# Attention and experts in one block on one core: the experts' buffers over the attention's, batch 6 routed between two projections, the next batch's projections three places later

## The chip, the cores and the metric

One core of one Trainium2 chip runs the whole program. The metric is the device time of one execution in microseconds (us), as the median of repeated runs; lower is better. The core has five engines with their own instruction streams: TensorE (PE, with its weight loads shown apart as PEld), VectorE (DVE), ScalarE (ACT), GpSimd (POOL) and SyncE (SP), which here only issues DMAs. The streams meet at semaphores.

## The reference

Batches are counted from 0 to 7. Per batch, 256 image rows and 128 text rows of 256 numbers are the 384 tokens:

```python
h = tok(x)                       # 3x3 colour matrix, curve of 16 points, weighted sum, clip to 0..1
h = concatenate([h, txt], axis=1)            # (8, 384, 256)
h = h + attn(layernorm(h))
h = h + ffn(layernorm(h))
# attn: c = x W_DKV (64 wide); k = c W_UK; v = c W_UV; q = x W_UQ; 16 heads of 16
#       causal softmax(q k / 4) v, then W_O
# ffn:  router scores = softmax(x router_w), 8 experts, top 2 of each token;
#       each expert takes its first 384 tokens of the 1st choice and its first 384 of the 2nd,
#       y = gelu(xe w1[e]) w2[e] (256 -> 1024 -> 256), weighted by the score and added; plus bias
```

## The kernel before, in words

**Two blocks.** `build` makes the shared tensors and calls `front` (attention and routing of all eight batches) and then `experts`. Each of the two opens its own stack of SBUF buffers and its own `nc.Block()`, in which the five engines' programs stand. At the end of a block every engine drains and meets the others (line 131 of the profile, line 1405 at the end of the second block). The buffers of `front` are given back at its end, and `experts` takes the same memory.

**Turns.** `front` runs over turns `n` from -1 to 19, with `b = n // 2`: turns 2b and 2b+1 compute attention of batch b, half of the heads each (8 heads, four places `p` = 0 to 3 with two heads each). PE carries out, in place p of turn n: the scores of turn n+1 (`scores`, lines 579 and 580, read by DVE's row maxima, line 1081), the shifted transposed scores of turn n in three units (`shifted_scores`, lines 601 and 602, read by ACT's exponentials, lines 887 and 889), and at fixed places the sums with the values (`values`, 637), the contexts' transposes (`contexts_back` 649, `contexts_out` 656), W_O (`project`, 665, two pieces per batch, read by DVE's `residual`, 1115). The order of each engine is written out by hand; nothing is planned at build time.

**The next batch's chain.** Tokens of batch b+2 go through colours and curve (DVE 1124 to 1156, in places 0 and 1 of even turn 2b), layer norm (DVE `norms`, `variances`, the root on POOL at line 477, DVE `scaled` 1178 in place 3), transposes (`tokens_back`, PE 673, ACT 936: half 0 at the end of even turn 2b place 3, half 1 in place 0 of turn 2b+1), the latent (`latents`, 680, ACT 940, place 0), and for four half heads' worth of queries and keys `query_key` in three stages (PE 695 or 697, then 700 twice). Each stage waits for ACT's bf16 copy of the one before it (948); these copies go by DMA from SP into the stacked tensors `qs` and `ks` (358). All of it shares PSUM bank 1. Those stacks are first read by `scores` in turn 2b+3.

**Routing.** Batch b-2 is routed in turn 2b and 2b+1: `router` (PE 727) in place 1 of the even turn, `choose` on DVE (1207 to 1213), `mark` on DVE in place 2 (one-hot rows and running counts, 1224 to 1230), `ranks` on PE in place 3 (738, 739: how many earlier tokens chose the same expert), `keep_ranks` on DVE (1217), then in place 0 of the odd turn `weigh` (1239 to 1251) and `place` (1255 to 1261), which gives each token its two slots, and six indirect DMAs from POOL (`send`, 494) that write the token's row into `slot_rows` in DRAM. For batches 6 and 7 there is no attention beside it: turns 16 to 19 hold the rest, with `turning` (745), multiplications whose result nobody reads, between the steps. Batch 7's project and second layer norm run in turns 16 and 17 and batch 6's `weigh` and `place` follow them on DVE in turn 17.

**The experts.** Units u = 0 to 15 are (expert u // 2, choice u % 2). SP loads the 384 rows of a unit from `slot_rows` (1462), PE transposes them (1616), ACT and DVE split them into a high and a low float32r part (1537, 1582), PE multiplies by w1 (1630: high x high, low x high, high x low), ACT applies gelu twice (1542, 1545), DVE forms the low part (1588), PE multiplies by w2 (1645), ACT scales (1553), and POOL adds the rows to the output by indirect DMA (1511). The weights of expert 0 are loaded into `wr` during the attention; their high part is made by ACT (1560), their low part by DVE (1594) and POOL (1518); those of the later experts wholly on POOL (1496, 1499). SP loads unit 0's rows when all sends but batch 7's last three have landed (semaphores `sent`), unit 1's to 3's after those (`sent_last`). PE's program is `transpose_rows(0)`, `transpose_rows(1)` (which waits for DVE's `xl` of unit 0), then `hidden(0, f)`.

Of the kernel before, what the change touches and what calls it, by code (L numbers as in the profile page):

```python
# [11 lines left out]

# [53 lines left out]
RANK_STEP = 14  # L66
# [4 lines left out]
NMAT = MAT_WO + KC * DIM + KC * E  # L71

# [6 lines left out]
def build(nc, x, txt, params, mats, w1, w2, out):  # L79
# [3 lines left out]
    with ExitStack() as ctx:  # L83
        def sb(name, shape, dt=F32, where=None):
            return (where or ctx).enter_context(nc.sbuf_tensor(name, shape, dt))
# [6 lines left out]
        w_in = [ctx.enter_context(nc.semaphore(f"w_in{i}")) for i in range(2)]  # L92

        sent = [ctx.enter_context(nc.semaphore(f"sent{q}")) for q in range(2)]
        sent_last = ctx.enter_context(nc.semaphore("sent_last"))
        res_out = ctx.enter_context(nc.semaphore("res_out"))

        common = (ident, banks, s_bank, t_bank, sb)
        routed = (sent, sent_last, res_out)
        front(nc, common, wr, w_in, routed, x, txt, params, mats, w1, w2, slot_rows, out)  # L100
        experts(nc, common, wr, w_in, routed, w1, w2, slot_rows, out)


def front(nc, common, wr, w_in, routed, x, txt, params, mats, w1, w2, slot_rows, out):
# [8 lines left out]
    ident, banks, s_bank, t_bank, sb = common  # L113
# [17 lines left out]
    with ExitStack() as own:  # L131
        def buf(name, shape, dt=F32):
            return sb(name, shape, dt, own)

        def sem(name):
            return own.enter_context(nc.semaphore(name))

        hid = buf("hid", [P, B, NT, DIM])
        ident_b = buf("ident_b", [P, P], BF16)
        minus_b = buf("minus_b", [P, P], BF16)  # L140
        mask_q = buf("mask_q", [P, P], BF16)
        mask_k = buf("mask_k", [P, P], BF16)
        eps_t = buf("eps_t", [P, NT])
        neg_half = buf("neg_half", [P, NT])
        flag_f = buf("flag_f", [1, 2])
        flag_i = buf("flag_i", [1, 1], I32)
        prm = buf("prm", [P, NPRM])
        bias = prm[:, NPRM - DIM:NPRM]
        ccm_t = prm[:, 0:9]
        cbias = prm[:, 9:12]  # L150
        shift_t = prm[:, 12:60]
        slope_t = prm[:, 60:108]
        conv_t = prm[:, 108:111]
        convb_t = prm[:, 111:112]
        curve_w = buf("curve_w", [P, CH * PTS])
        minus_s = buf("minus_s", [P, CH])
        warm = buf("warm", [P, NT])
        less = buf("less", [P, MPARTS * HALF * T // P], BF16)
        mat = buf("mat", [P, NMAT])
        dkv = mat[:, 0:KC * P].rearrange("p (c n) -> p c n", c=KC)  # L160
        uq = mat[:, KC * P:KC * P + KC * DIM].rearrange("p (c n) -> p c n", c=KC)
        uk = mat[:, MAT_UK:MAT_UK + DIM]
        uv = mat[:, MAT_UK + DIM:MAT_WO]
        wo = mat[:, MAT_WO:MAT_WO + KC * DIM].rearrange("p (c n) -> p c n", c=KC)
        rw = mat[:, MAT_WO + KC * DIM:NMAT].rearrange("p (c e) -> p c e", c=KC)

        xin = [wr[q][:, 0:CH * IT * W].rearrange("p (c j w) -> p c j w", j=IT, c=CH) for q in range(2)]
        acc = wr[0][:, IT * W * CH:NW].rearrange("p (j w) -> p j w", j=IT)
        g = buf("g", [P, CH, IT, W])
        r = buf("r", [P, CH, IT, W])  # L170
        stats = buf("stats", [P, NT, 6])
        mv = buf("mv", [P, NT, 2])
        ve = buf("ve", [P, NT])
        rstd = buf("rstd", [P, NT])
        xn = buf("xn", [P, NT, DIM])
        xnT = buf("xnT", [P, KC, T])
# [149 lines left out]
        def bank_of(key):  # L326
            if key == "C":
                return C
# [1374 lines left out]
```

## Time and profile before

| what | us |
|---|---|
| median of 3 runs (716.57, 717.54, 721.19) | 717.54 |
| profiled execution, its own time | 715.48 |
| span of that execution in the trace | 713.6 |
| mean granted TensorE clock in it | 0.977 |

Times of rows are microseconds from the span's start. A row of a timeline has start, length, engine, line, operation, output and input, count, and in square brackets the idle time of the engine ahead of it with what ended it. PE rows overlap, since matmuls are pipelined.

### The profile page before, as it was taken

What the parts mean: (1) busy time and instruction counts of PE and PEld (TensorE: products, weight loads), DVE (VectorE), ACT (ScalarE), POOL (GpSimd) and SP (SyncE); (2) the same over time, 40 slices, a digit from 0 to 9 for tenths busy, and PEclk for the clock granted to TensorE, in tenths of its full rate; (3) what the DMA queues carried; (4) which work ended last, traced back from release to release, by engine and by line L of the source; (5) the groups of instructions that cost most, each with busy time, mean ns of one, the idle gap of its engine ahead of it and who ended that gap; (6) DMA issues with size and microseconds to landing.
All of it is one profiled execution on the core that took longest, in us unless ns stands there. A gap on an engine that the chain in (4) does not pass through costs nothing. (4 is left out here: it accounts for less than half of the span.)

```text
span 713.6 us, 14553 instructions
## 1 busy us (share of the span) xinstructions
PE 647.0 (91%) x5574; PEld 543.9 (76%) x5574; DVE 401.1 (56%) x1005; ACT 378.1 (53%) x800; POOL 303.8 (43%) x401
## 2 busy tenths in 40 slices
PE   2797999989899898999989869999999999999992
PEld 2555666666667666667767869999999999999992
DVE  4886685777867687648765144444444444444320
ACT  4365766747567485565661065545554444555540
POOL 3300001003121131030423659877788888888233
PEclk9999999999999998999999979999999999999997
DMA  7448392604333043153102252444444444442223
GB/s 256 112 117 227 89 271 69 198 32 137 106 83 113 9 113 90 44 151 128 63 24 76 76 202 66 104 104 104 105 104 105 104 104 104 105 104 46 24 29 37
DMA packets 66477, 73.76 MB, mean 103 GB/s; under 512 B 6312, under 2 KB 61458, under 8 KB 66408
## 3 DMA queue, kind: packets, MB, share of 16 engines
q1 hardware_dynamic: 55584, 59.27, 27.6%
q0 software_dynamic: 9504, 13.00, 10.7%
q8 instruction: 44, 0.72, 0.5%
q10 hardware_dynamic: 1320, 0.57, 0.3%
q14 instruction: 25, 0.20, 0.1%
HBM read 31.62 MB, written 22.35 MB: 76 GB/s over the span
## 5 line engine op out<-in xcount | busy, mean ns | idle before, releaser
L1588 DVE TENSOR_TENSOR hl<-h,hh 128x384 fp32r<-128x384 f32 x128 | 103.8, 812 | 155.2 <-ACT h L1545 155.2
L1081 DVE TENSOR_REDUCE mx<-s_bank 128x2 f32<-128x256 f32 (+2 forms) x192 | 124.4, 684 | 56.6 <-PE s_bank L580 55.5
L1542 ACT ACTIVATE hh<-t_bank 128x384 fp32r<-128x384 f32 x128 | 63.0, 492 | 132.5 <-PE t_bank L1630 130.2
L889 ACT ACTIVATE pt<-t_bank 128x512 f32<-128x512 f32 x128 | 76.5, 598 | 68.0 <-PE t_bank L602 65.4
L1511 POOL DMA_INDIRECT out<-yo,xr x48 | 75.1, 1564 | 71.3 <-ACT yo L1553 61.6
L1499 POOL TENSOR_TENSOR wl<-wr,wh 128x256 fp32r<-128x256 f32 x112 | 94.2, 875 | 1.2
L1630 PE MATMUL t_bank<-xh,wh 128*128 128x384 f32 x256 | 86.6, 338 | 0.0
L601 PE MATMUL t_bank<-qs,ks 98*128 98x384 bf16 (+2 forms) x384 | 85.7, 275 | 0.6 <-ACT pt L887 0.4
L1630 PE MATMUL t_bank<-xl,wh 128*128 128x384 f32 x256 | 86.2, 337 | 0.0
L1630 PE MATMUL t_bank<-xh,wl 128*128 128x384 f32 x256 | 86.0, 336 | 0.0
L579 PE MATMUL s_bank<-ks,qs 96*128 96x128 bf16 (+2 forms) x384 | 78.7, 274 | 5.0 <-DVE mx L1081 4.0
L494 POOL DMA_INDIRECT slot_rows<-row,slot_i x48 | 47.7, 994 | 71.6 <-ACT pt L889 58.3
L580 PE MATMUL s_bank<-mask_q,ident_b 128*128 128x128 bf16 x384 | 74.7, 220 | 0.0
L1645 PE MATMUL bank<-wh,hh 128*128 128x256 f32 x256 | 72.9, 285 | 0.0
L1645 PE MATMUL bank<-wh,hl 128*128 128x256 f32 x256 | 72.0, 281 | 0.0
L1645 PE MATMUL bank<-wl,hh 128*128 128x256 f32 x256 | 71.8, 281 | 0.0
L602 PE MATMUL t_bank<-mask_k,ident_b 128*128 128x128 bf16 x384 | 68.4, 220 | 0.0
L1545 ACT ACTIVATE h<-t_bank 128x384 f32<-128x384 f32 x128 | 62.4, 488 | 0.1
L475 POOL TENSOR_TENSOR ve<-mv,eps_t 128x3 f32<-128x3 f32 x8 | 1.5, 190 | 127.9 <-DVE mv L1171 127.9
L601 PEld LDWEIGHTS t_bank<-qs,ks 98*128 98x128 bf16 x384 | 37.8, 98 | 21.8 <-issue 5.3
L579 PEld LDWEIGHTS s_bank<-ks,qs 96*128 96x128 bf16 x384 | 37.5, 98 | 16.0 <-DVE mx L1081 4.6
L1630 PEld LDWEIGHTS t_bank<-xh,wh 128*128 128x128 f32 x256 | 48.9, 191 | 0.0
(191 smaller groups left out, 1451.8 us busy)
## 6 DMA issues: line engine op xcount, KB each, us to landing
wr<-in_w SPq DMA_DIRECT2D x16, 1024.0 KB, 5.8
qs<-part SPq DMA_DIRECT2D x96, 96.0 KB
ks<-part SPq DMA_DIRECT2D x90, 96.0 KB
slot_rows<-empty SPq DMA_DIRECT2D x4, 1560.0 KB, 9.1
xr<-slot_rows SPq DMA_DIRECT2D x16, 390.0 KB, 3.3
wr<-in_x SPq DMA_DIRECT2D x8, 768.0 KB, 5.6
out<-hid SPq DMA_DIRECT2D x8, 384.0 KB, 3.5
qs<-mT ACTq DMA_DIRECT2D x64, 3.0 KB
```

Of the source, the lines that this page charges most:

```text
L579: pe.matmul(dst, q[0:MROW, h, j * P:(j + 1) * P], k[0:MROW, h, 0:w], start=True, stop=False)
L580: mm = pe.matmul(dst[:, j * P:(j + 1) * P], ident_b[:, :], mask_q[:, :], start=False, stop=True)
L601: pe.matmul(bank[:, col:col + w], k[:, h, j * P:(j + 1) * P], q[:, h, j * P:T], start=True, stop=False)
L602: mm = pe.matmul(bank[:, col:col + P], ident_b[:, :], mask_k[:, :], start=False, stop=True)
L889: ins = act.activation(pt[:, p, unit // 2, 0:AT[1]], bank, ACT.Exp)
L1081: ins = dve.tensor_reduce(mx[:, p // 2, j, 2 * (p % 2):2 * (p % 2) + 2], pair_region(s_bank, j), AX_X, ALU.max)
L1499: m = pool.tensor_tensor(wl[i][q][:, cols], wr[i][:, cols], wh[i][q][:, cols].bitcast(F32), ALU.subtract)
L1511: pool.indirect_dma_start(out=out, out_offset=bass.IndirectOffsetOnAxis(ap=xr[u % NX][:, t, DIM:DIM + 1].bitcast(I32), axis=0), in_=yo[u % ...
L1542: act.activation(hh[:, f, :], h_banks[f % NH], ACT.Gelu_apprx_tanh)
L1588: dve.tensor_tensor(hl[:, f, :], h[f % 2][:, :], hh[:, f, :].bitcast(F32), ALU.subtract).then_inc(hl_done, 1)
L1630: m = pe.matmul(h_banks[f % NH], w[:, c, cols], xx[:, c, :], start=(i == 0), stop=(i == len(parts) - 1))
L1645: m = pe.matmul(y_banks[t], hx[:, f, rows], w[:, f, :], start=(f == 0 and i == 0), stop=(f == FC - 1 and i == 2))
```

## The change

Both parts now hand back a tuple of five functions, and `build` makes one block in which each engine runs the first part's function and then the second's. The large buffers of the attention are taken from a stack that is closed before `experts` takes its own, so that these lie over them. The waits at the end of SP's program for `w_in` and `zeroed` are gone with the block.

```diff
+        with ExitStack() as attention:
+            def lent(name, shape, dt=F32):
+                return attention.enter_context(nc.sbuf_tensor(name, shape, dt))
+
+            before = front(nc, common, lent, wr, w_in, routed, ...)
+        behind = experts(nc, common, wr, w_in, routed, ...)
+        block = ctx.enter_context(nc.Block())
+
+        @block.sync
+        def _(sp):
+            before.sync(sp)
+            behind.sync(sp)
...
+    qs = [[lent(f"qs{q}{h}", [SROWS, HALF, T], BF16) for h in range(2)] for q in range(2)]
...
-            for i in range(2):
-                sp.wait_ge(w_in[i], 16)
-            sp.wait_ge(zeroed, 16 * (PIECES + 1))
```

`pt`, `vb`, `g`, `r`, `xn`, `xnT`, `cx`, `cxn`, `cn`, `ks` and `part` are lent in the same way. POOL's addition of the bias is cut into three:

```diff
-                pool.tensor_tensor(hid[:, b, :, :], hid[:, b, :, :],
-                                   bias.rearrange(...).to_broadcast([P, NT, DIM]), ALU.add).then_inc(res_done, 1)
+            for t in range(NT):
+                pool.tensor_tensor(hid[:, b, t, :], hid[:, b, t, :], bias, ALU.add).then_inc(res_done, 1)
```

PE (the tests on `late` and `live` are left out where they are as before):

```diff
                 if p == 1:
-                    routed = not odd and live(b - 2)
+                    routed = live(b - 2) and n < OVER        # OVER = 16
+                    if routed and odd: ranks(b - 2)
+                    elif routed: router(b - 2)
...
                 if p == 3:
-                    routed = not odd and live(b - 2) and n != OVER
-                    if routed: ranks(b - 2)
+                    if not odd and b - 2 == B - 1: ranks(b - 2)
                     if cur: contexts_back(n, 0, ...)
-                if odd and p == 0: tokens_back(b + 2, 1, 1)
-                if odd and p: query_key(b + 2, p - 1, 1)
-                if not odd and p == 0: query_key(b + 1, 3, 1)
+                if odd and p == 1: latents(b + 2, 1)
+                if odd and p >= 2: query_key(b + 2, p - 2, 2)
+                if not odd and p < 2: query_key(b + 1, 2 + p, 2)
                 ... shifted_scores(n, p, 1), scores(n + 1, p, 1)
-                if odd and p: query_key(b + 2, p - 1, 2)
-                if not odd and p == 0: query_key(b + 1, 3, 2)
+                if odd: tokens_back(b + 2, 0, 1) if p == 0 else query_key(b + 2, p - 1, 0)
+                if not odd and p == 0: query_key(b + 1, 3, 0)
                 ... values
-                if odd and p == 0: latents(b + 2, 1)
                 ... project(b - 1, 0)
                     if p == 3 and n == OVER:
-                        project(b - 1, 1); ranks(b - 2); turning(60)
+                        ranks(b - 2); project(b - 1, 1); turning(50)
                 ... shifted_scores(n, p, 2)
-                if odd: query_key(b + 2, p, 0)
+                if odd: tokens_back(b + 2, 1, 1) if p == 0 else query_key(b + 2, p - 1, 1)
+                if not odd and p == 0: query_key(b + 1, 3, 1)
...
-                if n == LAST - 2 and p == 1: turning(40)
-                if n == LAST - 2 and p == 3: turning(220)
-                if p == 3 and live(b + 2): tokens_back(b + 2, 0, 1)
+                if n == LAST - 2 and p == 1: turning(24)
+                if n == LAST - 2 and p == 3: turning(160)
```

ACT's copies follow the same places: `tokens_back(b + 2, 1)` and each `query_key` of stage 1 ahead of the first exponential of the next place, stage 2 behind it, stage 0 behind the second. On DVE:

```diff
                 odd turns
-                if p == 0 and n != OVER + 1: weigh(b - 2); place(b - 2)
+                if p == 0 and n < OVER: weigh(b - 2)
+                if p == 0 and b - 2 == B - 1: place(b - 2)
+                if p == 1 and n < OVER: keep_ranks(b - 2); place(b - 2)
                 if p == 0: residual(b - 1, 1)
                 if p == 1: norms2(b - 1); variances2(b - 1)
                 if p == 1 and n == OVER + 1: keep_ranks(b - 2)
+                                             place(b - 2)
                 if p == 2: scaled2(b - 1); last_residual
-                if p == 2 and n == OVER + 1: weigh(b - 2); place(b - 2)
                 even turns
-                if p == 2: mark(b - 2)
+                if p == 2 and n >= OVER: mark(b - 2)
-                if p == 3 and n != OVER: keep_ranks(b - 2)
+                if p == 3 and b - 2 == B - 1: weigh(b - 2); keep_ranks(b - 2)
                 if p == 3: scaled(b + 2)
+                if p == 3 and n == OVER: weigh(b - 2)
                 if p == 3: residual(b - 1, 0)
+                if p == 3 and n < OVER: mark(b - 2)
```

The copy of the running count (`seen`, line 1251) moves from `weigh` to the end of `keep_ranks`. The work inside each function is otherwise the same, and so is all of the second part.

## Rows read from the trace of the kernel before

**Rows 1.** Stretches: busy us per engine (count), granted clock, DMA share, GB/s
```profile
236.80:240.20 3.40, 3.40 (x12) 2.72 (x10) 2.73 (x10) 0.58 (x1) 1.36 (x2) 0.50 0.11 39
281.00:288.00 7.00, 6.33 (x30) 4.95 (x31) 4.81 (x19) 0.60 (x1) 2.11 (x3) 0.51 0.06 20
410.90:421.10 10.20, 4.34 (x17) 3.97 (x18) 3.72 (x4) 5.93 (x7) 1.89 (x1) 0.50 0.77 260
421.10:689.00 267.90, 267.90 (x1911) 267.41 (x1911) 115.54 (x141) 136.06 (x309) 204.04 (x267) 1.00 0.40 90
```
**Rows 2.** Line groups of PE from 40 to 378: busy, mean ns, idle before
```profile
L738 PE MATMUL bank<-ohb,tri 128*128 128x16 bf16 x18 | 1.7, 173 | 6.4 <-DVE seen L1230 4.8 <-issue 1.6
L673 PE MATMUL t_bank<-ident,xn 128*128 128x128 f32 x36 | 6.5, 289 | 4.0 <-DVE xn L1178 4.0
L579 PE MATMUL s_bank<-ks,qs 96*128 96x128 bf16 x366 | 75.2, 274 | 3.7 <-DVE mx L1081 3.7
L700 PE MATMUL t_bank<-part,minus_b 128*128 128x384 bf16 x52 | 17.4, 334 | 3.6 <-ACT part L948 3.5
```
**Rows 3.** Timeline of PE: the first matmul of ranks, batches 0 and 3
```profile
145.83 0.17 PE L738 MATMUL bank<-ohb,tri 128*128 128x16 bf16 x1 [1.63 <-issue]
...
281.67 0.19 PE L738 MATMUL bank<-ohb,tri 128*128 128x16 bf16 x1 [1.59 <-DVE seen L1230]
```
**Rows 4.** Timeline of PE: the same key projection in three successive batches
```profile
206.29 0.89 PE L697 MATMUL t_bank<-ckvT,mat 128*128 128x384 f32 x2 [0.33 <-ACT part L948]
...
252.24 0.88 PE L697 MATMUL t_bank<-ckvT,mat 128*128 128x384 f32 x2 [0.33 <-ACT part L948]
...
299.50 0.88 PE L697 MATMUL t_bank<-ckvT,mat 128*128 128x384 f32 x2 [0.33 <-ACT part L948]
```
**Rows 5.** Instructions of line 131, the first block's end: ns, first and last start
```profile
L131 POOLq DRAIN  x1: 10838/10838/10838, 400.5 to 400.5; - x1
```
**Rows 6.** The chain that ended last, 340 to 420: start, length
```profile
411.70 3.04 DMA xr<-slot_rows
...
414.78 1.56 PE s_bank L1616 x6
...
416.36 0.82 ACT xh L1537
...
418.30 1.51 PE s_bank L1616 x6
```
**Rows 7.** Landings of POOL's twelve sends (line 494), 385 to 416
```profile
DMA to landing us min/median/max: 2.3/2.6/3.4
```
**Rows 8.** Timeline, DVE's slots and POOL's sends of batches 6 and 7
```profile
390.83 0.17 DVE L1261 CAST slot_i<-slot_f 128x6 int32<-128x6 f32 x1
...
391.80 1.04 POOL L494 DMA_INDIRECT slot_rows<-row,slot_i  x1 [5.08 <-DVE slot_i L1261]
...
397.20 0.17 DVE L1261 CAST slot_i<-slot_f 128x6 int32<-128x6 f32 x1
...
405.91 0.97 POOL L494 DMA_INDIRECT slot_rows<-row,slot_i  x1 [0.30 <-issue]
```
**Rows 9.** Timeline of DVE: keep_ranks of batches 6 and 7, end of batch 7's weigh
```profile
385.40 0.17 DVE L1217 TENSOR_TENSOR ranked<-s_bank,oh 128x48 f32<-128x48 f32 x1
...
394.92 0.21 DVE L1217 TENSOR_TENSOR ranked<-s_bank,oh 128x48 f32<-128x48 f32 x1 [1.16 <-PE s_bank L739]
...
396.30 0.35 DVE L1251 COPY seen<-seen 128x16 bf16<-128x16 bf16 x1
```
**Rows 10.** Timeline: PE's last turning; DVE's part of w1 in the experts
```profile
394.74 12.44 PE L745 MATMUL t_bank<-ident_b 128*128 128x128 bf16 x220
...
412.73 2.36 DVE L1594 TENSOR_TENSOR wl<-wr,wh 128x1024 fp32r<-128x1024 f32 x2 [15.35 <-ACT wh L1560]
```
**Rows 11.** Instructions of line 1511 in the experts: ns min/median/max
```profile
L1511 POOL DMA_INDIRECT out<-yo,xr x48: 1551/1561/1632, 447.1 to 705.4; - x48
```
**Rows 12.** The page: POOL's bias addition
```profile
L487 POOL TENSOR_TENSOR hid<-hid,prm 128x768 f32<-128x768 f32 x7 | 13.2, 1885 | 2.0 <-DVE row L1201 2.0
```

More of the change, by code:

```diff
@@ L13 @@
+from collections import namedtuple
 from contextlib import ExitStack
@@ new lines, in front @@
+    mv2 = buf("mv2", [P, NT, 2])
+    ve2 = buf("ve2", [P, NT])
+    rstd2 = buf("rstd2", [P, NT])
+    row = [buf(f"row{q}", [P, NT, ROW]) for q in range(2)]
+    rowT = buf("rowT", [P, KC, T])
+    logits = buf("logits", [P, NT, E])
+    top = buf("top", [P, NT, 8])
+    top_i = buf("top_i", [P, NT, 8], U32)
+    top_f = buf("top_f", [P, NT, TOPK])
+    shifted = buf("shifted", [P, NT, E])
+    expd = buf("expd", [P, NT, E])
+    ssum = buf("ssum", [P, NT])
+    rsum = buf("rsum", [P, NT])
+    etop = buf("etop", [P, NT, TOPK])
@@ new lines, in front @@
+    oh = buf("oh", [P, NT, TOPK, E])
+    ohb = buf("ohb", [P, NT, KE], BF16)
+    seen = buf("seen", [P, NT + 1, KE], BF16)
+    pick = buf("pick", [P, NT, TOPK, E])
+    ranked = buf("ranked", [P, NT, TOPK, E])
+    rank = buf("rank", [P, NT, TOPK])
+    first = buf("first", [P, NT, TOPK])
+    full = buf("full", [P, NT, TOPK])
+    slot_f = buf("slot_f", [P, NT, TOPK])
+    slot_i = [buf(f"slot_i{q}", [P, NT, TOPK], I32) for q in range(2)]
+    qs = [[lent(f"qs{q}{h}", [SROWS, HALF, T], BF16) for h in range(2)] for q in range(2)]
@@ new lines, in part_key, with stack_count, stack @@
+    def part_key(b, k):
+        return EARLY_BANKS[b][k] if b < EARLY else 1
+    def stack_count(b, half):
+        return 16 * (NL * (b + 1) - (len(K_PARTS) if half == 0 else 0))
+    def stack(queue, b, k, stage, landed=None):
+        half, s = k // 2, k % 2
+        dst = (ks if s else qs)[b % 2][half]
+        queue.wait_ge(*part_made(b, k, stage))
+        if b >= 2 and stage == 0:
+            queue.wait_ge(t_ready, 12 * (2 * (b - 2) + half + 1))
+        for at, piece in enumerate(K_PARTS if s else Q_PARTS):
+            if piece == stage:
+                queue.dma_start(dst[at:MROW:len(Q_PARTS)], part[k][stage][:, :]).then_inc(landed or stack_in[half], 16)
@@ new lines, in experts @@
+    w_split = [sem(f"w_split{i}") for i in range(2)]
+    w_first = [sem(f"w_first{i}") for i in range(2)]
+    x_in = [sem(f"e_x_in{i}") for i in range(NX)]
+    x_ps = sem("x_ps")
+    xh_done = sem("xh_done")
+    xl_done = sem("xl_done")
+    w_high = [sem(f"w_high{i}") for i in range(2)]
+    h_ps = sem("h_ps")
+    gelu_done = sem("gelu_done")
+    hl_done = sem("hl_done")
+    y_ps = sem("y_ps")
+    y_sb = sem("y_sb")
+    added = sem("added")
+    h_banks = [t_bank[:, 0, 0:CAP], t_bank[:, 1, 0:CAP], t_bank[:, 2, 0:CAP]]
@@ new lines, in first_high @@
+                act.activation(wh[i][0][:, cols], wr[i][:, cols], ACT.Copy).then_inc(w_first[i], 1)
+        first_high(0)
+        rows(0)
+        first_high(1)
+        rows(1)
+        for f in range(FC):
+            hidden(0, f)
+        for u in range(U):
+            for f in range(FC):
+                if u + 1 < U and f < FC - 1:
+                    hidden(u + 1, f)
+                if u + 2 < U and f == ROWS_AT:
+                    rows(u + 2)
+            results(u)
+            if u + 1 < U:
+                hidden(u + 1, FC - 1)
```

2610 lines of the change are left out of this document (1276 added, 1334 removed).

## The prediction

> **What bounds the kernel now.** I read the stretches first: granted clock and busy time. From 421.1 to 689.0 PE is busy for 267.9 of 267.9 us at full clock (2.4 GHz) [rows 1]. The change leaves the experts' own work as it is, so this stretch and the tail behind it can only move as a whole: what counts is when `hidden(0, 0)` begins. Ahead of it lie the attention, in which PE is nearly full, and the handover, in which it is not.
>
> For the attention I read the line groups of PE from 40 to 378: the last column tells which instruction PE stood before, and for whom. Three entries matter: 6.4 us before `ranks` (line 738), 4.0 us before the transposes of `xn` (673), and 3.7 us before the scores, for the row maxima (579); another 3.6 us stands before the second and third stages of the query and key projection (700) [rows 2]. The timeline says where the 6.4 us lie: in four batches, 0 to 3, with 1.63 us the first time and 1.59 us the last [rows 3]. Those are the turns in which DVE also has a curve to do. Then the period: the same key projection comes at 206.29, 252.24 and 299.50 [rows 4]. The first matmuls of `ranks` of batches 0 and 3 are (281.67 - 145.83) / 3 = 45.3 us apart [rows 3], with one stretch at half clock among them.
>
> For the handover I read line 131, the chain and POOL's sends. POOL's sequencer reaches the end of the block at 400.5 and drains for 10.84 us, to 411.3 [rows 5]; SP's load of the first unit's rows goes out at 411.70, after it [rows 6]. The last send begins at 405.91 [rows 8], and a send lands 2.3 to 3.4 us after its start, 2.6 in the median [rows 7], so about 408.5. Some 3.2 us at least are waited for nothing but the meeting of the engines.
>
> **The change, part by part.**
>
> *Ranks later (attention).* `mark` moves behind `residual` and `ranks` to place 1 of the next turn. DVE has then a whole place for `mark`, and the 1.6 us per batch are gone: -6.4 us in all [rows 2, 3]. Because `variances` no longer waits behind `mark` on DVE, the layer norm of the next batch is ready sooner too. Cost: `keep_ranks`, the copy of `seen` and `place` come into place 1 of the odd turn, ahead of `norms2`. From the end of `keep_ranks` in the last turn DVE needed to 397.37 for `weigh` and `place`, 2.2 us, of which about 1 us is `place` [rows 8, 9]; so `norms2` starts some 1.4 us later. POOL's root, `scaled2` and `rows_back` hang on it; PE reaches `rows_back` only in place 3, so the place between covers the 1.4 us. If that cover fails it costs up to 1.4 us x 6 batches = 8.4 us; this is the bad end, and 0 the good one. I take 0.5 us.
>
> *The chain three places later.* `tokens_back` comes after DVE's `scaled` by a place rather than right behind it: -4.0 us [rows 2]. The stages then stand at other distances: stage 0 to 1 has only one unit of shifted scores between them, where before it was stage 2 to the next stage 0 that had only one. So the short gap (0.33 us of idle at line 697 [rows 4]) changes place, and the 3.6 us before line 700 stay in the main. Bounds: all 3.6 us gone, or the same again added; I take 0, with 0.5 us for something new. Everything the step issues moves with it, the 12 copies on ACT and 24 stacking DMAs from SP included. SP's queue behind them holds `load_x`, `store` and the load of expert 0's weights; the stacks are first read in turn 2b+3, one whole turn (half of 45 us [rows 3]) after the last of half 0's is made, so the delay of three places, 17 us, leaves over 5 us and is covered; if not, see the fourth rival.
>
> *The 3.7 us before the scores* [rows 2] come from `choose` and the curve on DVE in place 1, which stay: 0.
>
> *The clock.* Between 236.8 and 240.2, and from 281.0 to 288.0, PE ran at half clock (1.2 GHz) [rows 1], the second of them from within a stall before line 738, which ended at 281.67 [rows 3]; the first one has another such stall ahead of it. What it cost is in the period: 299.50 - 252.24 = 47.26 us and 252.24 - 206.29 = 45.95 us [rows 4], against a period without a slow stretch. That one follows from 281.67 - 145.83 = 135.84 [rows 3]: these are three periods, of which one, 45.95, has the first slow stretch in it, so an undisturbed one lasts (135.84 - 45.95) / 2 = 44.95. The two stretches cost 1.0 and 2.3 us. With the stalls ahead of them gone I hold it for somewhat likelier than not that neither stretch comes: -3.3 us; the other end is 0.
>
> The Trainium skill, page "TensorE: Matmul & The Clock Gate" (Terms), prices slow time as the time throttled times (1 - K/N), half of it here. By that rule the 10.4 us of rows 1 would have cost 5.2 us, and the sum would be 1.9 us better; the periods say 3.3, since part of that time PE would have been waiting anyway, and the sum goes by the periods.
>
> *POOL's bias addition in three.* One took 1.885 us, seven of them 13.2 us [rows 12]. Three of a third each cost between the same and, by two more starts, some tenths more; POOL has idle time behind it, and the next waiter is a send, which nobody awaits for several places. 0 us; were it the other way, a few tenths at most.
>
> *The handover.* Batch 6: `weigh` now runs while PE projects batch 7, and `place` directly behind `keep_ranks`, which ended at 385.57 [rows 9]. With 1 us for `place` its slots stand at 386.6 rather than 391.0 [rows 8], before `scaled2` of batch 7 can start. Its six sends, one every 1.275 us ((405.91 - 391.80) / 11 [rows 8]), then run from 387.4 to 395. `weigh` and `ranks` of batch 6 stand ahead of `residual` of batch 7: 0.3 us lost. Batch 7: `weigh` fills the 1.16 us that DVE waited for PE at 394.92 [rows 9], and the shorter `turning` (24 for 40) lets `ranks` start when its input is there: 1.0 us gained in all. So its slots stand at 397.37 + 0.3 - 1.0 = 396.7, and its sends, no longer behind batch 6's, start 0.8 us later (as 391.80 behind 391.00 [rows 8]) at 397.5 and the last at 397.5 + 5 x 1.275 = 403.9, where it was 405.91.
>
> Then, without the meeting: the third send starts at 400.1 and lands at 402.7; unit 0's rows are loaded (3.04), transposed (1.56), split by ACT (0.82) and then by DVE (1.1 with the hop, from 417.18 to the next transposes at 418.30) [rows 6], by 409.4. The last send lands at 403.9 + 2.6 = 406.5; unit 1's rows are there 0.1 + 3.04 later, at 409.7, and their transposes (1.51) end at 411.2. In the kernel before those ended at 419.8 [rows 6]. Difference -8.6 us. Expert 0's w1 is split on ACT and DVE (2.36 us there [rows 10]) beside the sends, long before. w2's low part on POOL follows ACT as before, 8 to 9 us earlier too, and `result(0, 0)` asks for it 9 us after `hidden(0, 0)`. Against this stands the clock: `turning(160)` takes 160 x 12.44 / 220 = 9.0 us [rows 10], from 394 to 403, and PE then waits 3 us, works 1.5, waits 2.5. At the handover before, PE had half clock for 10.2 us, the first 1.7 of `hidden` included [rows 1]; now more of `hidden` may fall into such a stretch: I give 0.5 us, with -0.8 and +2 as ends. Handover: -8.1 us. Its ends: if only the 3.2 us of the meeting and the 2.0 us of earlier sends come, -5.2; at the best -9.5.
>
> The Trainium skill, page "SBUF — State Buffer" ("SBUF: two separate sides"), speaks against running DVE beside POOL's sends: their descriptors are written through a port pair that some DVE operations lock, and the send then stands until they end. DVE's two subtractions of w1 (2.36 us [rows 10]) would now fall on batch 7's sends and put the last one at 406.3, so by that rule the sum would be 2.4 us worse. In the experts POOL's sends run beside DVE's subtractions of the same kind and take 1551 to 1632 ns all 48 of them [rows 11], so I leave the sends at their length and keep the rule as a rival.
>
> *Sum.* -6.4 - 4.0 + 0.5 + 0.5 - 3.3 - 8.1 = -20.8 us. Against the profiled execution's 715.48 that is 694.7; the median of the runs shown, 717.54, lies 2.1 us above it, and the same step from there gives 696.7 us.
>
> **The rivals.**
>
> 1. *The slow stretches stay* or come elsewhere. For: there are four such stalls and two such stretches [rows 1, 2], so the stalls alone don't bring them. Against: both lie behind stalls. Time: 696.7 + 3.3 = 700.0.
> 2. *The locked port.* The sends of batch 7 stand behind DVE's subtractions: 696.7 + 2.4 = 699.1. For: both run at the same time only now. Against: rows 11.
> 3. *The stalls come back elsewhere.* PE loses before the scores or `rows_back` what it gained before `ranks` (DVE has the same work in the same turn, only in another order); 1.4 us per batch, 8.4 us, and no fewer slow stretches: 696.7 + 8.4 + 3.3 = 708.4. For: PE stood for DVE in three of the four groups shown [rows 2], so DVE is never far behind. Against: DVE's whole work is unchanged, and PE's stops for it were at fixed places that the change moves.
> 4. *The stacks are late*: the other side. If the delayed chain's stacking DMAs land after PE asks for them in turn 2b+3, PE stalls at each batch's first scores. From where it decides: a lag of the last half-0 stack of over a turn, 22.5 us, behind its place. Price: to be slower than before it has to cost over 20.8 / 6 = 3.5 us per batch; 4 us per batch gives 717.54 + 3.2 = 720.7, and then over 1% slower only from 5 us per batch on. For: SP issues 24 stacks per batch one after another. Against: over 5 us are left.
> 5. *The meeting wasn't the limit.* The rows would be late anyway, and the handover gives only the 2.0 us of earlier sends: 696.7 + 6.1 = 702.8.
>
> **How the numbers follow.** Chances: forecast 0.45, rival 1 0.18, rival 2 0.08, rival 3 0.17, rival 4 0.04, rival 5 0.08. The range runs from 691 (forecast with the 3.6 us before line 700 gone and the best handover) to 708, just short of rival 3, so that about 2 in 10 are left out. About 1%, 7.2 us, is what a measurement of this kernel can tell from no change: faster by more (below 710.4) takes in all but rival 4 and the worse half of 3: 0.92; within 1% 0.05; slower 0.03.
>
> **What would show it.** Right: the group of line 738 without idle time, line 673 without DVE; the same key projection every 44.95 - 1.6 - 0.5 = 42.9 us in the batches with curves; no stretch of clock 0.50 in the attention; no drain between send and load; the load of unit 0's rows before the last send; `hidden(0, 0)` at about 419.5 - 20.8 = 398.7. Wrong: more than 6 us of idle before line 579 or 715; sends longer than 1.1 us or landing after over 3.4; a first `hidden` later than 405.

## The result, and the profile after

The changed kernel takes 704.83 us (median of 4 runs, 704.80 to 706.88) against 717.06 of the kernel before, measured beside it: a ratio of 0.983, 95% interval 0.980 to 0.986, or -12.2 us where -20.8 was forecast. The profiled executions are 704.81 and 715.48, -10.7; their spans, 703.1 and 713.6, are -10.5 apart, and the account below is of the spans. In the changed file the lines named stand 24 to 30 further down (738 is 763, 579 is 604, 494 is 520).

Four points of the timeline and its end cut the two spans into stretches with the same work in each (us; the last column is the change of the stretch that ends at this point; what the runs' handover takes, below, is the stretch from the second point to the third):

| point | before | after | change |
|---|---|---|---|
| PE's first matmul of line 602 (627 after), in the first shifted scores | 45.81 | 45.14 | -0.7 |
| end of the attention's last shifted scores | 374.33 | 368.61 | -5.0 |
| end of the second rows' transposes (PE can go on with `hidden`) | 419.82 | 405.38 | -8.7 |
| start of POOL's last send to `out` | 705.40 | 692.36 | +1.4 |
| end of the span | 713.60 | 703.07 | +2.5 |

The handover gave 8.7 us, where the prediction has 8.6 without its clock term, and the attention 5.0 where with the clock 12.7 were forecast. Behind the handover 3.9 us were lost: 1.4 for which the prediction has 0.5 (the clock over the first `hidden`), and 2.5 of which it says nothing.

*Attention.* The line groups of PE from 40 to 378, after (busy, mean ns, idle before; as [rows 2]):

```profile
L763 PE MATMUL bank<-ohb,tri 128*128 128x16 bf16 x18 | 1.6, 169 | 1.0 <-ACT cx L939 0.8
L698 PE MATMUL t_bank<-ident,xn 128*128 128x128 f32 x36 | 6.0, 276 | 0.1
L604 PE MATMUL s_bank<-ks,qs 96*128 96x128 bf16 x366 | 74.9, 273 | 4.2 <-DVE mx L1111 4.2
L725 PE MATMUL t_bank<-part,minus_b 128*128 128x384 bf16 x52 | 17.3, 332 | 5.8 <-ACT part L978 5.8
L722 PE MATMUL t_bank<-ckvT,mat 128*128 128x384 f32 x24 | 10.6, 524 | 4.1 <-ACT part L978 4.1
L635 PE MATMUL bank<-ident_b,ms 128*8 128x128 bf16 x93 | 10.2, 218 | 4.8 <-DVE hid L1145 3.6 <-ACT vb L987 1.0
```

The first four rows answer to the four of [rows 2] in their order: `ranks` from 6.4 to 1.0 and the transposes of `xn` from 4.0 to 0.1, as forecast. But line 725 has 5.8 for 3.6, and two groups grew that the prediction had no number for. In the trace of before they read:

```profile
L697 PE MATMUL t_bank<-ckvT,mat 128*128 128x384 f32 x24 | 10.6, 524 | 2.4 <-ACT part L948 2.3
L610 PE MATMUL bank<-ident_b,ms 128*8 128x128 bf16 x93 | 10.2, 219 | 1.2 <-ACT vb L957 1.0 <-DVE hid L1115 0.2
```

That is 4.1 for 2.4 and 4.8 for 1.2. The six groups hold 21.3 us before and 20.0 after: 9.3 us of waits went and 8.0 came. The same key projection as in [rows 4] now comes every 44.57 and 44.56 us (timeline of PE):

```profile
206.16 0.56 PE L722 MATMUL t_bank<-ckvT,mat 128*128 128x384 f32 x1 [0.34 <-ACT part L978]
250.73 0.56 PE L722 MATMUL t_bank<-ckvT,mat 128*128 128x384 f32 x1 [0.34 <-ACT part L978]
295.29 0.88 PE L722 MATMUL t_bank<-ckvT,mat 128*128 128x384 f32 x2 [0.36 <-ACT part L978]
```

The undisturbed period was 44.95, so 0.4 us of it are gone and not 2.1. Of the attention's 5.0 us the clock is 3.3, by the prediction's periods. Both stretches of [rows 1] are at full clock (stretches of after: span, busy us and count of PE, PEld, DVE, ACT and POOL, granted clock, DMA share, GB/s; then the handover and the experts):

```profile
236.80:240.20 3.40, 2.66 (x39) 1.74 (x38) 3.23 (x12) 2.13 (x4) 0.00 (x0) 1.00 0.00 1
281.00:288.00 7.00, 6.26 (x74) 4.48 (x72) 5.84 (x26) 3.69 (x9) 0.00 (x0) 1.00 0.06 20
399.60:409.80 10.20, 7.48 (x27) 7.11 (x28) 3.22 (x3) 6.21 (x9) 4.64 (x2) 0.50 0.69 233
409.80:687.00 277.20, 277.20 (x1991) 276.70 (x1989) 115.60 (x141) 137.09 (x313) 205.65 (x269) 1.00 0.40 89
```

Where a wait of 0.74 us per batch before line 635 comes from, DVE's timeline says:

```profile
234.45 0.68 DVE L1111 TENSOR_REDUCE mx<-s_bank 128x2 f32<-128x512 f32 x1
...
235.51 0.36 DVE L1139 TENSOR_TENSOR cxn<-bank,rs 128x192 f32<-128x192 f32 x1
235.78 1.05 DVE L1208 TENSOR_SCALAR xn<-hid,mv,rstd 128x256 f32<-128x256 f32 x3
236.75 0.68 DVE L1145 TENSOR_TENSOR hid<-hid,bank 128x512 f32<-128x512 f32 x1
```

and PE's, with the instruction that waited for it:

```profile
237.58 0.33 PE L635 MATMUL bank<-ident_b,ms 128*8 128x128 bf16 x3 [0.74 <-DVE hid L1145]
```

DVE has all but no gap here: from the start of `choose` at 226.16 through the curve, the maxima and `scaled` to the end of `residual` it stands idle once, for 0.34 us behind its own curve. PE needs the bank that `residual` (line 1145) reads. Before, the 1.6 us stall ahead of `ranks` lay in front of this wait, and gave DVE the time; `residual` itself then waited 0.83 us for PE's `project` (at 240.59 in before).

*Handover.* POOL's sends of batches 6 and 7, first and last, and DVE's part of w1 beside them:

```profile
381.87 1.04 POOL L520 DMA_INDIRECT slot_rows<-row,slot_i  x1 [0.64 <-issue]
...
391.08 1.19 POOL L520 DMA_INDIRECT slot_rows<-row,slot_i  x1 [1.73 <-DVE slot_i L1290]
...
397.69 0.97 POOL L520 DMA_INDIRECT slot_rows<-row,slot_i  x1 [0.30 <-issue]
```
```profile
390.21 2.35 DVE L1619 TENSOR_TENSOR wl<-wr,wh 128x1024 fp32r<-128x1024 f32 x2
```

The last send starts 8.22 us earlier than in [rows 8], 2.5 of them gained since the last shifted scores. DVE's subtractions run from 390.21 to 392.56 over the first send of batch 7, which takes 1.19; the five behind it take 0.97 as in [rows 8]. Then the chain, where the load goes out with no meeting before it [rows 5, 6]:

```profile
397.19 3.10 DMA xr<-slot_rows
...
400.34 1.55 PE s_bank L1640 x6
...
403.86 1.51 PE s_bank L1640 x6
405.38 10.41 PE t_bank L1654 x48
```

*Experts and end.* Half clock, which before covered the first 1.7 us of `hidden`, now lasts to 409.8 and covers 4.8 us of it. The first 48 matmuls of `hidden` took 10.41 us, where before they took 8.99: +1.4. The last loss is in the instructions of the block's end, after and before:

```profile
L87 POOLq DRAIN  x1: 6442/6442/6442, 696.4 to 696.4; - x1
...
L1405 POOLq DRAIN  x1: 3972/3972/3972, 709.4 to 709.4; - x1
```

Before, the last DRAIN stands behind a block that had sent 48 indirect DMAs; now one block has sent 96. That is the +2.5.

### The profile page after: what moved, and what is told of

It is laid out like the page before. It is cut to its first block, busy times and chain, and to the rows that moved or that the text cites. A ratio compares the mean times of both kernels' runs of the same rounds, so it can differ in the third digit from the quotient of the medians.

```text
span 703.1 us, 14382 instructions
## 1 busy us (share of the span) xinstructions
PE 639.8 (91%) x5488; PEld 533.9 (76%) x5488; DVE 400.3 (57%) x1005; ACT 377.8 (54%) x800; POOL 305.5 (43%) x415
## 4 chain that ended last, share of the span: by engine, by line
PE 67%; DVE 12%; ACT 7%; issue 5%; DMA 3%; SPq 3%; POOL 1%; ACTq 0%; DVEq 0%; POOLq 0%
PE t_bank L1654 19%; PE bank L1669 12%; PE s_bank L1669 6%; PE bank L662 5%; DVE mx L1111 3%; PE t_bank L626 3%; PE t_bank L720 3%; SPq L392 3%; PE s_bank L604 3%; ACT part L978 2%; PE bank L690 2%; PE s_bank L1640 2%; DVE wr L1166 2%; PE t_bank L627 1%; PE s_bank L605 1%
## 5 line engine op out<-in xcount | busy, mean ns | idle before, releaser
L1111 DVE TENSOR_REDUCE mx<-s_bank 128x2 f32<-128x256 f32 (+2 forms) x192 | 122.6, 683 | 51.9 <-PE s_bank L605 51.3
L978 ACT ACTIVATE part<-t_bank 128x384 bf16<-128x384 f32 x78 | 38.1, 488 | 29.0 <-PE t_bank L720 16.9
```

Of the source, the lines that this page charges most:

```text
L1111: ins = dve.tensor_reduce(mx[:, p // 2, j, 2 * (p % 2):2 * (p % 2) + 2], pair_region(s_bank, j), AX_X, ALU.max)
```

## The experiments

The runs stood on two chips. Runs e1 to e4, b_third, e3_again, e4_again and e9 are on one, on which the kernel before takes 733.6 us in the first group and 729.9 in the second; a_again and e5 to e7 on one where it takes 718.4. The profiles of before and after have no chip on record; by their times they belong to the latter, the faster one. Only runs of one group are compared by their times, otherwise ratios to before or stretches of the profiles.

**e1, one block and nothing else.** The orders of before (with the edits of e3 and e4 below, and the last turns' as well), its `turning` and its bias addition, in the changed kernel's single block.

```diff
...
-            for t in range(NT):
-                pool.tensor_tensor(hid[:, b, t, :], hid[:, b, t, :], bias, ALU.add).then_inc(res_done, 1)
+            pool.tensor_tensor(hid[:, b, :, :], hid[:, b, :, :],
...
-                        turning(160)
+                        turning(220)
```

> The block alone: one block with the buffers laid over each other, every engine's order and the lengths of turning as in the kernel before. Theory A (the block pays at the handover and gives part of it back): the last send stays at about 405.9, unit 0's rows go out 3 sends earlier, the second transposes end 6 us earlier (about 413.8 for 419.8), the slow clock costs 1 us more of hidden, and POOL's drain at the end takes 6.4 us for 4.0: 717.1 - 6.0 + 1.2 + 2.5 = 714.8. Theory B (the drain at the end is unrelated to the block): 712.3. Theory C (the whole gain of the change is the block): 704.8.

Measured: 725.18 us, ratio 0.991 (0.987 to 0.995): 8.4 us less than before in its group, where theory A had 2.3. Which stretch gives them isn't shown, since before has no profile on that chip. It isn't the handover: e1's takes 49.1 us, where before's took 45.5 (on the other chip) and e2's, with two blocks, 44.3. SP issues the first load at 413.26, and PE takes the rows up only at 422.74. The timeline of PE has its own `turning` in between:

```profile
401.87 1.73 PE L772 MATMUL t_bank<-ident_b 128*128 128x128 bf16 x28
404.61 0.39 PE L772 MATMUL t_bank<-ident_b 128*128 128x128 bf16 x4 [1.01 <-issue]
...
416.64 6.26 PE L772 MATMUL t_bank<-ident_b 128*128 128x128 bf16 x109 [0.49 <-issue]
```

The 220 matmuls, 12.4 us in [rows 10], take 21 us with seven stops, 5.6 us together, in which PE waited for nothing that the profile shows. Filler work in front of the rows is then what the rows wait for, and in this profile the single block gains nothing at the handover as long as the filler isn't cut with it.

**e2, the changed orders in two blocks.**

```diff
+            run(attention.enter_context(nc.Block()), before)
...
-            behind.sync(sp)
+        run(ctx.enter_context(nc.Block()), behind)
```

> The new orders alone, with two blocks again and the meeting between them. Theory A: attention 5.7 us and batch 7's sends 2.5 us earlier, the drain in the middle back and the one at the end at 4.0 us again: 717.1 - 8.2 = 708.9. Theory C (the orders bring nothing without the block): 717.

Measured: 715.89 us, ratio 0.976 (0.973 to 0.979), where theory A amounts to 0.989 (708.9 of 717.1). So on this chip the orders alone bring 17.7 us and not 8.2; why so much more than on the other is open. The handover takes 44.3 us; one block on that chip needs 39.4 (b_third), 39.3 (e3) and 39.5 (e3_again). So the single block is worth 4.9 us there. Its last DRAIN:

```profile
L87 POOLq DRAIN  x1: 3972/3972/3972, 710.4 to 710.4; - x1
```

3.97 again, beside 6.44 in all ten profiles with one block and no added DRAIN. So the block costs 2.5 us at the end for the 4.9 that it gives.

**e3, the chain back at its old places**, first without the changed kernel beside it, then with it.

```diff
-                if odd and p == 1 and late(b + 2):
-                    latents(b + 2, 1)
...
+                    if p == 3 and live(b + 2):
+                        tokens_back(b + 2, 0, 1)
```

> The kernel after, with the next batch's chain at its old places and the late ranks kept. Theory A (the late chain brings nothing: the transposes stood for DVE's scaled, and now the maxima stand for DVE's residual, both behind the same row of DVE work; and its new places cost 0.64 us per batch before the projection's stages): period 0.4 to 0.6 us shorter than the 44.57 of the kernel after, 702 to 704. Rival (the late chain was worth its 4 us): 707 to 709.

> The changed kernel with the chain of the next batch at its old places, beside the changed kernel itself. Prediction's step (the chain removes 0.67 us of stalls per batch, gives 0.08 back): period of the full batches 0.5 to 0.7 us longer, the kernel 3 to 4 us slower than the changed one. Rival from the trace of after, that DVE's unbroken work from the choice to the residual holds the period and the chain's places only choose where TensorE waits: period within 0.2 us and the kernel within 1 us of the changed one.

Measured: 715.14 us, ratio 0.974 (0.972 to 0.977); again 712.31, beside 712.38 for the changed kernel (b_third, ratio 0.975, 0.969 to 0.981). PE's groups from 40 to 378 of e3_again:

```profile
L698 PE MATMUL t_bank<-ident,xn 128*128 128x128 f32 x36 | 6.6, 291 | 7.3 <-DVE xn L1202 7.3
L722 PE MATMUL t_bank<-ckvT,mat 128*128 128x384 f32 x24 | 10.6, 524 | 2.3 <-ACT part L973 2.3
L635 PE MATMUL bank<-ident_b,ms 128*8 128x128 bf16 x93 | 10.2, 219 | 1.2 <-ACT vb L982 1.0 <-DVE hid L1139 0.2
```

and of b_third:

```profile
L698 PE MATMUL t_bank<-ident,xn 128*128 128x128 f32 x36 | 6.0, 276 | 0.1
L722 PE MATMUL t_bank<-ckvT,mat 128*128 128x384 f32 x24 | 10.6, 524 | 4.0 <-ACT part L978 4.0
L635 PE MATMUL bank<-ident_b,ms 128*8 128x128 bf16 x93 | 10.2, 218 | 4.8 <-DVE hid L1145 3.7 <-ACT vb L987 1.0
```

With the chain at its old places PE waits 7.2 us more for `xn`, and 1.7 and 3.6 less at the other two. The first batch without a slow stretch in either takes 45.09 (chain back) and 45.17 us, the next 45.22 and 45.65 (from the first shifted scores of an even turn to those of the next even one). Up to the last shifted scores e3_again is 2.1 us ahead of b_third, whose attention has one stretch at half clock and e3_again's none. The move gains nothing, and may cost a little, less than the 0.4 to 0.6 us per batch of the first expectation: DVE's unbroken work ends with `scaled` and `residual`, and PE waits for the one or the other.

**e4, the ranks back at their old places** in the attention, likewise twice.

```diff
-                    if p == 1 and live(b - 2) and n < OVER:
-                        keep_ranks(b - 2)
...
-                    if p == 2 and live(b - 2) and n >= OVER:
+                    if p == 2 and live(b - 2):
                         mark(b - 2)
...
+                    if p == 3 and live(b - 2) and n < OVER:
+                        keep_ranks(b - 2)
```

> The kernel after, with mark, ranks, keep_ranks and place at their old places in the attention (turns below 16), the late chain kept. Theory A (the stall before ranks returns at 1.6 us and the 0.74 us before the maxima go, since DVE works on meanwhile): 4 batches x 0.9 us = 3.5 us longer, 708.3, and up to 711.6 if half clock comes again in the attention. Rival (DVE's row of work is the limit in any order): within 1 us of 704.8.

> The changed kernel with mark, ranks, keep_ranks and place of the attention at their old places, beside the changed kernel itself. Prediction's step (1.59 us before the ranks go, 0.5 in all comes back): period of the batches that route 1.0 to 1.6 us longer, five such batches, and the stretches at half clock again: 5 to 10 us slower than the changed kernel. Rival: the wait before the ranks is back (1.6 us per batch) while the 0.74 us before the maxima goes, so the period is 0.8 to 0.9 us longer and the kernel 4 to 5 us slower.

Measured: 722.74 us, ratio 0.986 (0.983 to 0.989); again 718.98, 6.6 us over b_third. PE's groups of e4_again (one line further down):

```profile
L764 PE MATMUL bank<-ohb,tri 128*128 128x16 bf16 x18 | 1.7, 172 | 6.4 <-DVE seen L1261 4.8 <-issue 1.6
L636 PE MATMUL bank<-ident_b,ms 128*8 128x128 bf16 x93 | 10.2, 218 | 2.3 <-DVE hid L1145 1.2 <-ACT vb L987 1.0
```

The 6.4 us of [rows 2] are back to the tenth, and 2.5 us before the maxima go in exchange. The stalls of batches 1 to 3 last 1.59 us each and end at 191.19, 238.43 and 285.69; half-clock stretches begin at 191.4, 239.2 and 287.0, 0.2 to 1.3 us after a stall's end, where b_third has a single one, at 259.3 (stretches of e4_again, columns as above):

```profile
191.40:194.80 3.40, 3.40 (x19) 2.82 (x16) 2.39 (x7) 0.60 (x1) 2.12 (x3) 0.50 0.11 39
239.20:242.60 3.40, 3.40 (x14) 2.79 (x12) 2.85 (x11) 0.60 (x1) 1.68 (x2) 0.50 0.11 39
287.00:290.40 3.40, 3.40 (x11) 2.46 (x10) 2.67 (x11) 0.35 (x1) 1.13 (x2) 0.50 0.12 42
```

PE is busy all through them. What one costs, the two profiles of this kernel show: e4_route_back has the first two stretches and not the third. The period with the third (from odd turn to odd turn) is 47.28 us for 45.60, half the stretch's length, but the last shifted scores end at 378.35 for 377.31, only 1.0 us later: part of the loss is made up before that. Up to the last shifted scores e4_again is 4.1 us behind b_third, of which two more stretches at this price are 2.1. The stalls themselves, 6.4 us of idle time in the view, are worth the remaining 2.0 (an estimate, since it takes b_third's own stretch at the same price). The first period with such a stall and no slow stretch is 46.34 us where b_third has 45.17. The other 2.5 us of the 6.6 arise behind that point, mostly up to `rows_back` of batch 7 (16.0 us where b_third needs 13.8), as the last turns get shifted against each other.

**a_again and b_third, the changed kernel** as a yardstick in its group.

> The changed kernel as it is, on the chip on which the runs e1 to e4 stood beside the kernel before. All theories: its ratio to before is that of the first chip, 0.983 (0.980 to 0.986), and POOL's last DRAIN takes 6.4 us. It is the yardstick for e5 to e7, which go to the same chip.

> The changed kernel once more, as the yardstick on this chip for e3, e4 and e9. All theories: ratio to before 0.979 to 0.986 if this chip is like the one of the first comparison.

Measured: 704.54 us, ratio 0.981 (0.979 to 0.984), and 712.38, ratio 0.975 (0.969 to 0.981), below the 0.979 that was expected. The first wasn't on the chip of e1 to e4, as its expectation has it; the second was.

**e5, two DRAINs of POOL ahead of the last one**, in turn 9 of the attention and behind row group 13 of the experts.

```diff
+                if n == 9:
+                    pool.drain()
...
+            if u == 14:
+                pool.drain()
```

> The changed kernel with a DRAIN of POOL in the attention's last turn but one and one behind row group 13 of the experts. If the cost of the last DRAIN grows with the indirect DMAs sent since the drain before (3.97 us after 48 in before, 6.44 us after 96 in after: some 0.05 us each on 1.5), the last one, with 4 to 8 sends behind the drain before it, takes 1.7 to 2 us and the kernel gets 4 to 4.7 us faster than the changed one (ratio to it 0.993 to 0.994). If a DRAIN at the end costs the same whatever was sent, or the added ones hold POOL's sends back, it is the same or slower by up to 10 us.

Measured: 699.81 us, 4.7 less than a_again; ratio to before 0.974 (0.972 to 0.975). The three DRAINs:

```profile
L583 POOLq DRAIN  x1: 3905/3905/3905, 257.4 to 257.4; - x1
...
L1555 POOLq DRAIN  x1: 10625/10625/10625, 664.8 to 664.8; - x1
...
L87 POOLq DRAIN  x1: 534/534/534, 698.0 to 698.0; - x1
```

(Turn 9 is a middle one of the attention; "the last turn but one" in the expectation is wrong.) The last DRAIN is down from 6.44 to 0.53 us, more than the straight line through 3.97 and 6.44 gave. Of these 5.9 us the kernel shows 4.7; its handover takes 38.1 us for the 36.9 of a_again. The long one of 10.6 us begins with two of its group's sends still to run, the last of them until 669.3, and ends at 675.5; POOL's next send comes at 680.93, for an output of ACT, so it is held up by nothing of this.

**e6, both new waits of a period at once**: `project` and `residual` earlier, ACT's copies ahead of the colours.

```diff
+                if not odd and p == 3 and live(b - 1) and n < OVER:
+                    project(b - 1, 0)
...
+                if odd and p in (1, 2) and late(b + 2):
+                    query_key(b + 2, p - 1, 1)
```

> The changed kernel with its two new waits of a period taken on: DVE's residual ahead of scaled and the project that TensorE issues behind shifted put ahead of it (against the 0.74 us before the maxima), and ScalarE's copies of query_key and tokens_back ahead of the colours (against the 0.68 us before L725). Theory that the period is held by these two places: each goes from the list of idle times, 0.7 to 1.4 us per batch over six batches, 4 to 8 us faster than the changed kernel. Rival, that DVE's unbroken work from the choice to the residual sets the period: the idle time turns up before the scores or the shifted copies instead, and the time is within 1 us of the changed kernel's.

Measured: 707.41 us, ratio 0.984 (0.982 to 0.987), 2.9 us worse than a_again. The waits have moved to a neighbour (timeline of PE):

```profile
212.68 1.53 PE L720 MATMUL t_bank<-xnT,mat 128*128 128x384 f32 x4 [0.80 <-ACT part L979]
...
237.83 0.33 PE L635 MATMUL bank<-ident_b,ms 128*8 128x128 bf16 x3 [0.84 <-DVE hid L1148]
```

The middle periods stay at 44.55 us. `project` ahead of the scores delays these, and DVE now waits 0.92 us for them (the maximum starts at 235.67). That is the rival's outcome as far as the waits and the periods go (not in the time, which is 2.9 us longer and not within 1), but my edit, not DVE's work, made it.

**e7, PE kept busy through the handover.**

```diff
-                        turning(160)
+                        turning(214)
...
+        for _ in range(32):
+            pe.matmul(t_bank[:, 2, 0:P], ident[:, :].bitcast(BF16)[:, 0:P], ident[:, :].bitcast(BF16)[:, 0:P], start=True, stop=True)
```

> The changed kernel with 54 more turning matmuls in the handover and 32 small ones between the two groups' transposes, so that TensorE does not stand idle before the experts. If the half clock over the first hidden units (10.41 and 11.67 us beside 8.99 and 10.24 in before) comes from the 5.1 us of idle time around the first transposes, the half-clock stretch ends before hidden or is gone, and the time is 1.4 to 2.4 us lower than the changed kernel's. If it stays, or if the added matmuls delay the transposes by more, it is the same or up to 1 us slower.

Measured: 704.60 us beside 704.54. Both sides of it happened (the chain of e7):

```profile
398.50 4.17 DMA slot_rows<-row,slot_i
402.69 3.90 DMA xr<-slot_rows
406.58 0.04 issue
406.63 0.88 PE s_bank L1640 x6
407.51 8.58 PE t_bank L1654 x48
```

At full clock the first `hidden` takes 8.58 us, 1.6 less than the 10.22 of a_again, but it starts 1.8 us later: 0.6 us because a half-clock stretch of 6.8 us, where a_again has one of 3.4, slows the router ahead of the ranks (2.01 us for 1.51), 1.9 because the last send's landing and the load took 4.17 and 3.90 us for the 3.08 and 3.12 of a_again, less 0.7 for transposes at full clock. Why the DMAs were slower, and whether the longer clock stretch has to do with the edit, which stands behind it in PE's order, no run shows.

**e9, `residual` ahead of `scaled`, alone**, with e5's two DRAINs.

```diff
-                    if p == 3 and live(b + 2):
-                        scaled(b + 2)
...
                     if p == 3 and live(b - 1):
                         residual(b - 1, 0)
+                    if p == 3 and live(b + 2):
+                        scaled(b + 2)
```

> The changed kernel with the two DRAINs of e5 and DVE's residual ahead of scaled, TensorE's order untouched. Theory that DVE's unbroken work up to the residual sets the period: the residual ends 0.96 us earlier, the 0.74 us before the maxima go, the period falls from 44.55 to between 43.8 and 44.3, over six batches 2 to 4 us on top of e5, ratio to before 0.968 to 0.971. Rival, as in e6: TensorE waits as long elsewhere (tokens_back's xn is 0.7 us later), the period stays 44.55 and the ratio is e5's 0.974.

Measured: 701.96 us, ratio 0.961 (0.954 to 0.967); 10.4 us less than b_third in the same group. DVE's timeline:

```profile
190.18 0.68 DVE L1147 TENSOR_TENSOR hid<-hid,bank 128x512 f32<-128x512 f32 x1
190.77 1.05 DVE L1210 TENSOR_SCALAR xn<-hid,mv,rstd 128x256 f32<-128x256 f32 x3
```

PE's groups:

```profile
L637 PE MATMUL bank<-ident_b,ms 128*8 128x128 bf16 x93 | 10.2, 219 | 1.5 <-ACT vb L989 1.0 <-DVE hid L1147 0.2 <-ACT rowT L993 0.2
L700 PE MATMUL t_bank<-ident,xn 128*128 128x128 f32 x36 | 6.0, 276 | 0.1
```

and its last DRAIN takes 0.53 us again. The wait is gone (1.5 for 4.8) and has not come back before the transposes of `xn`. Periods in which neither run has a slow stretch fall by 0.8 us, from 45.17 to 44.37 and from 44.98 to 44.16; the end of the last shifted scores comes 3.8 us earlier, with one slow stretch in the attention of each run. Of the 9.5 us between the two spans the attention has these 3.8 and the last DRAIN 5.9. This is the fastest version against before.

## Why the prediction was right in its sign and wrong in its size

- *Ranks later, -6.4 + 0.5.* The mechanism stands: `ranks` lost its wait, `norms2` hurt nobody. The size doesn't: I took 6.4 us of PE's idle time as time of the kernel. e4_again gives some 2.0 us for it in the attention without the clock, since DVE's `scaled` and `residual` were due right behind. Rival 3 described just that, but put the new wait before the scores or `rows_back`; it came before the maxima.
- *The chain, -4.0 + 0.5.* Wrong. e3_again shows no gain within its measurement (ratio 0.977, 0.970 to 0.985, beside 0.975). The step that failed is "-4.0 us": the wait for `xn` went and as much came before the maxima, `ckvT` and line 725, where I had taken 0 for a change of the short gaps. That the stacks were late (rival 4) isn't seen.
- *The clock, -3.3.* Both stretches went, in after and in a_again. What ties them to the stalls before `ranks` is the count: the four profiles of kernels with these stalls (before, e1, both of e4) have nine slow stretches between 100 us and the end of the attention, each beginning inside one of the sixteen stalls or up to 1.3 us behind it; the ten profiles without the stalls have four, all on the slower chip. The size is less sure. The first stretch of [rows 1] cost 1.0 us by the periods though PE was busy for all of its 3.4 us, so my reason, that PE would have waited anyway, fits only the second. By the rule of the Trainium skill, page "TensorE: Matmul & The Clock Gate" (Terms), half of the time throttled is lost, 1.7 us of 3.4. The two profiles of e4 agree with it within the period (1.7), and show 1.0 at the end of the attention.
- *Attention as a whole*: forecast 12.7, measured 5.0, of which 3.3 are the clock.
- *Bias in three*: no run has it alone. 21 additions take 15.1 us for the 13.2 of [rows 12]; in four batches POOL stands idle 1.1 to 2.0 us between them and the next send, and in two the send follows after 0.17 us, as before.
- *Handover, -8.1*, or -8.6 and the clock's +0.5. Measured -8.7 in the first pair, without the clock over `hidden`. Sends earlier: 2.5 (I had 2.0). The meeting and what hangs on it: 6.2 (I had 6.6); e2 gives 4.9 on the other chip, inside my ends. Rival 5 is out.
- *The locked port* (rival 2): the one send beside DVE's subtractions takes 1.19 us, those behind it 0.97, and the last starts at 397.69. The Trainium skill, page "SBUF — State Buffer" ("SBUF: two separate sides"), tells of locked-out descriptors for DVE operations in a 2-port mode, and has two inputs from SBUF lock only against a GpSimd operation that reads SBUF. My reading, that the rule holds in full for these subtractions, would have cost 2.4 us; the trace shows at most 0.2.
- *Clock in the handover, +0.5*: +1.4, within the +2 that I had as an end; with it the handover is -7.3 for -8.1. e7 shows that it is real (10.22 to 8.58) and why it isn't to be had this way.
- *Left out altogether*: POOL's DRAIN at the end of the span, +2.5. I read line 131's DRAIN as a wait of the handover and never asked what the same instruction does at the last block's end. e2 and e5 show it from both sides.

Added up: -0.7 (the start, unforecast) - 5.0 - 8.7 + 1.4 + 2.5 = -10.5.

That 704.83 lies between 691 and 708 is owed to the width of the range and not to the sum, whose 696.7 is 8.1 us off. The sum is off by 7.7 us in the attention, 0.9 in the clock of the handover and 2.5 in the DRAIN, all one way, against 0.7 at the start. The mechanism behind the 7.7 is mostly rival 3's, to which I gave 0.17. Without its clock part rival 3 gives 696.7 + 8.4 = 705.1; that this is so near is partly chance, since it holds neither the DRAIN nor the clock over `hidden`.

Of the signs on record, these came as forecast: no wait before `ranks` and `xn` to speak of, no stretch at half clock in the attention, no drain between send and load, and unit 0's load (397.19) ahead of the last send (397.69). The period is 44.56 and not 42.9, and `hidden(0, 0)` begins at 405.03 and not at 398.7, just over the 405 that I had set as a sign of being wrong; the one send of 1.19 us is over the 1.1 that was another such sign.

What stays open: the 0.7 us at the start; why the two chips differ by 2% on the kernel before and by 1% on the changed one, and why e1 and e2 gain more on the slower one than expected; PE's stops inside `turning` there; and what POOL's DRAIN pays for. No run separates the number of indirect DMAs since the last DRAIN from POOL's other work or the time since.

## What to carry to other kernels

Idle time before an instruction is worth removing only up to the next wait on the same engine: ask of the producer (here DVE) whether it has a gap before its next deadline, and if it has none, reorder by deadline (`residual` before `scaled`) instead of moving the consumer. A stall can still be worth removing for the clock that follows it. And when blocks are merged, read what each block's end did besides the meeting: two DRAINs added where POOL had nothing urgent to do gave 4.7 us.

## What the runs showed of the hardware

- POOL's DRAIN behind indirect DMAs: 3.97 us after 48 of them (before and e2), 6.44 after 96 (ten profiles, to the nanosecond), 0.53 at the end with eight sent since the start of the drain before (e5). It isn't a wait for landings: the last send has landed 0.2 us before the DRAIN begins, in before, after and e5 alike (709.18 and 709.4, 696.17 and 696.4, 697.75 and 698.0).
- Half clock came inside a 1.6 us stall of PE or up to 1.3 us after its end in nine of sixteen cases (before, e1, e4_route_back, e4_again); with stalls of 0.7 us in the same turn it came once in the attention (b_third) or not at all (after, a_again).
- A stretch of 3.4 us at half clock with PE busy throughout made its period 1.7 us longer and the end of the attention 1.0 us later (e4_again beside e4_route_back).
- PE's run of small matmuls stopped for 0.3 to 1.1 us at a time on one chip (e1, b_third) and not in the profile of before on the other.
